# Fifth first-layer passes of two blocks as two 64-row products side by side in the array

## The reference

```python
def _L0_ffn_ref(x, Wg, bg, W1, b1, W2, b2):       # x: normalized tokens
    gate_logits = jnp.einsum('bte,en->btn', x, Wg) + bg
    top = jnp.argmax(gate_logits, axis=-1)
    h = gelu(jnp.einsum('bte,neh->nbth', x, W1) + b1)      # E=192 -> H=768
    y = jnp.einsum('nbth,nhe->nbte', h, W2) + b2           # H=768 -> E=192
    onehot = one_hot(top, N_EXP)
    return jnp.einsum('nbte,btn->bte', y, onehot)
```

## Time and profile before

| | |
|---|---|
| Median of three runs | 170.0 us |
| The profiled execution's own time | 171.58 us |
| Its span, first to last instruction | 169.8 us |
| Granted TensorE clock, mean | 0.956 of full speed |
| Busy: TensorE / VectorE / ScalarE / GpSimd | 83% / 77% / 70% / 25% |
| Costliest group on TensorE | L1414, the up passes, 360 products, 29.7 us |

### The profile page before, as it was taken

One profiled execution on the slowest core, in us unless ns is written; L12 is line 12 of the kernel. 1 busy time (PEld: TensorE's weight loads), 2 busy tenths in 40 slices (PEclk: granted clock), 3 DMA queues, 4 the chain that ended last, 5 costly groups with the idle time before them and its releaser, 6 DMA issues.

```text
span 169.8 us, 5316 instructions
## 1 busy us (share of the span) xinstructions
PE 140.6 (83%) x1893; PEld 108.5 (64%) x1893; DVE 130.3 (77%) x401; ACT 119.0 (70%) x232; POOL 42.6 (25%) x104
## 2 busy tenths in 40 slices
PE   0499588997988969988999999714899999999960
PEld 0499577974555536555657557501389999999950
DVE  2727565999999997899999896879977676767660
ACT  8934447759799985999996775560277787778610
POOL 7212522351000030101011057274001222422242
PEclk9999999999999987999999999955799999999998
DMA  3799999999999999700000012133693100101010
GB/s 83 286 297 251 257 402 256 236 226 291 367 369 368 366 367 380 314 11 0 0 4 4 4 58 109 58 130 143 187 352 122 35 30 25 29 21 37 8 46 1
DMA packets 12921, 27.72 MB, mean 163 GB/s; under 512 B 1744, under 2 KB 8666, under 8 KB 12896
## 3 DMA queue, kind: packets, MB, share of 16 engines
q1 hardware_dynamic: 11744, 24.41, 46.0%
q0 software_dynamic: 1152, 2.97, 4.8%
HBM read 15.39 MB, written 12.29 MB: 163 GB/s over the span
## 4 chain that ended last, share of the span: by engine, by line
PE 50%; DVE 15%; ACT 13%; DMA 9%; issue 8%; SPq 4%; POOL 1%; DVEq 0%; ACTq 0%; POOLq 0%
PE lin_bank L1414 12%; DMA patches<-in_patches 9%; PE head_bank L1121 4%; PE head_bank L1435 3%; PE head_bank L1427 3%; PE head_bank L1428 3%; PE lin_bank L1448 3%; PE lin_bank L1281 3%; PE lin_bank L1258 2%; ACT vint L501 2%; ACT w L519 2%; PE lin_bank L1150 2%; PE score_bank L1175 2%; PE score_bank L1281 2%; ACT aT L547 2%
## 5 line engine op out<-in xcount | busy, mean ns | idle before, releaser
L638 ACT ACTIVATE q<-lin_bank,b 128x128 f32<-128x128 f32 x72 | 25.0, 368 | 7.2 <-PE lin_bank L1414 6.5
L1414 PE MATMUL lin_bank<-q,w 128*128 128x128 f16 x360 | 29.7, 219 | 0.3 <-ACT q L628 0.3
L1121 PE MATMUL head_bank<-proj_w,patches 128*128 128x192 f32 x84 | 17.5, 368 | 8.5 <-DMA patches<-in_patches 8.4
L1414 PEld LDWEIGHTS lin_bank<-q,w 128*128 x360 | 23.7, 98 | 0.8 <-issue 0.6
L1121 PEld LDWEIGHTS head_bank<-proj_w,patches 128*128 128x128 f32 x84 | 15.9, 217 | 9.1 <-issue 6.6
L1427 PE MATMUL head_bank<-early,q 128*128 x72 | 17.7, 246 | 0.1
L1435 PE MATMUL head_bank<-early,q 128*128 x72 | 17.7, 246 | 0.0
L1428 PE MATMUL head_bank<-early,q 128*128 x72 | 17.7, 246 | 0.0
L1083 DVE CAST q<-q 128x384 f16<-128x384 f32 (+2 forms) x25 | 8.8, 352 | 11.3 <-ACT q L638 11.2
L1154 PE MATMUL lin_bank<-xqT,ww1q 96*128 96x288 bf16 x96 | 15.4, 286 | 1.6 <-ACT vint L501 0.9
L501 ACT ACTIVATE vint<-lin_bank,fac 128x768 int16<-128x768 f32 x16 | 14.3, 903 | 3.1 <-PE lin_bank L1150 2.9
(11 more groups left out here) (172 smaller groups left out, 355.2 us busy)
## 6 DMA issues: line engine op xcount, KB each, us to landing
slots<-blank SPq DMA_DIRECT2D x3, 2938.0 KB, 22.6
patches<-in_patches SPq DMA_DIRECT2D x9, 384.0 KB, 13.1
early<-in_ww SPq DMA_DIRECT2D x3, 576.0 KB, 12.0
patches<-in_w SPq DMA_DIRECT2D x4, 384.0 KB, 12.2
patches<-in_w SPq DMA_DIRECT2D x8, 192.0 KB, 13.7
patches<-in_w SPq DMA_DIRECT2D x2, 576.0 KB, 13.0
v<-slots SPq DMA_DIRECT2D x5, 226.0 KB, 3.9
patches<-slots SPq DMA_DIRECT2D x4, 226.0 KB, 4.9
```

The lines of the kernel that those rows point to most:

```text
L638: a.activation(g[:, j % 2, m], up_bank[n % 4][:, 0:P], ACT.Gelu, scale=1.0 / WSCALE, bias=b1[:, bass.ds(e, 1), m]).then_inc(g_ok, 1)
L1121: last = mm(emb_bank[t][:, 0:E], patches[:, t, kc], proj_w[:, kc], start=kc == 0, stop=kc == KE - 1)
L1414: last = mm(up_bank[n % 4][:, 0:P], up_weights(j, part, m), xT[:, j % 3, piece], start=x == 0, stop=x == len(PASSES) - 1)
```

## The change

The fifth pass's zeros go. In the rows the doubled high tail and the zeros behind the low tail are dropped (388 words instead of 452), and with them ScalarE's second copy (L541) and GpSimd's memset (L402). `slots_T` now transposes the two heads as before, and each tail twice, as 128 x 64 pieces, to PSUM partitions 0 to 63 and 64 to 127: six transposes for four. So `xT` piece 2 is as before, and piece 3 holds the low tail in both halves. For tiles 0 and 1 the fifth pass stays a full product (which now also adds low by low). For tiles 2 to 11 the high tail weights of two blocks are laid on rows 0 to 63 and on rows 64 to 127 of a new tile `tails`; the fifth passes of blocks m-1 and m are issued together after the four full passes of block m (m = 1, 3, 5), as two products of 64 rows and 128 columns into two PSUM banks. The `up` of an even block therefore ends one block later. SyncE reads the expert numbers too, behind the load of tile 2, and copies the tail weights by two DMAs for each tile, between the loads of the slot tiles. Ten slot tiles instead of eight fit into the dead buffers.

```diff
--- before
+++ after
@@ -59,10 +59,11 @@
     CENTRE_AT, GATES_AT = 5, 12
     KEEP_FROM, KEEP_TO = 2, 12
     WAVES = [(0, 4), (4, 7), (7, TT)]
-    IDX = 2 * E + TAIL
+    IDX = 2 * E
     ROW = IDX + 4
-    HI, LO = 2 * E, 2 * E + 2 * P
+    HI, LO = 2 * E, 3 * E
     QG, VG = HB // 2, PPC
+    PAIRED = 2
 
     with ExitStack() as ctx:
         def sb(name, shape, dt=F32):
@@ -195,9 +196,13 @@
 
         values = v[:].rearrange("p b n -> p (b n)").bitcast(F32)
         keys = k[:].rearrange("p b m n -> p (b m n)").bitcast(F32)
-        homes = [values[:, x * ROW:(x + 1) * ROW] for x in range(5)] + [keys[:, x * ROW:(x + 1) * ROW] for x in range(3)]
+        homes = [values[:, x * ROW:(x + 1) * ROW] for x in range(6)] + [keys[:, x * ROW:(x + 1) * ROW] for x in range(4)]
         FREE_TILES = len(homes)
         homes += [flat[:, 4 * HID + x * ROW:4 * HID + (x + 1) * ROW] for x in range(SLOT_TILES - FREE_TILES)]
+
+        t0 = 4 * HID + (SLOT_TILES - FREE_TILES) * ROW
+        tails = flat[:, t0:t0 + (SLOT_TILES - PAIRED) * HID // 4].bitcast(F16).rearrange(
+            "p (j m n) -> p j m n", j=SLOT_TILES - PAIRED, m=HM // 2)
 
         def xs(j):
             return homes[j]
@@ -229,6 +234,7 @@
         w2_in = [sem(f"w2_in{e}") for e in range(NEXP)]
         patch_in = [sem(f"patch_in{t}") for t in range(TT)]
         ww1_in = [sem(f"ww1_in{s}") for s in range(3)]
+        tail_in = [sem(f"tail_in{j}") for j in range(PAIRED, SLOT_TILES)]
         xs_in = [sem(f"xs_in{j}") for j in range(SLOT_TILES)]
         pool_step, nought_ok, ident_ok, pad_ok, qpad_ok, blank_ok, const_ok, setup, scales_ok, psum_clear = map(sem, (
             "pool_step", "nought_ok", "ident_ok", "pad_ok", "qpad_ok", "blank_ok", "const_ok", "setup", "scales_ok", "psum_clear"))
@@ -374,6 +380,14 @@
                 if j == FREE_TILES:
                     sp.wait_ge(wlo_ok, EARLY)
                 sp.dma_start(xs(j), slots_d[bass.ds(at[j], P), :]).then_inc(xs_in[j], 16)
+                if j == PAIRED:
+                    sp.wait_ge(wlo_ok, EARLY)
+                    sp.wait_ge(expert_ok, 1)
+                    experts = load_experts(mybir.EngineType.SP)
+                if j >= PAIRED:
+                    part = w1[0:TAIL, bass.ds(experts[j], 1), 2].rearrange("p e (m b n) -> p (e m) b n", b=2, n=P)
+                    for b in range(2):
+                        sp.dma_start(tails[b * TAIL:(b + 1) * TAIL, j - PAIRED], part[:, :, b]).then_inc(tail_in[j - PAIRED], 16)
 
         @block.gpsimd
         def _(pool):
@@ -399,7 +413,6 @@
             gp.iota(blank[:, IDX:ROW].bitcast(I32), pattern=[[0, 4]], base=T, channel_multiplier=1).then_inc(blank_ok, 1)
             gp.iota(row[:, :, IDX:ROW].bitcast(I32), pattern=[[P, TT], [0, 4]], base=0,
                     channel_multiplier=1).then_inc(blank_ok, 1)
-            gp.memset(row[:, :, IDX - TAIL // 2:IDX], 0.0).then_inc(const_ok, 1)
             step(gp.memset(before[:], 1.0))
 
             gp.affine_select(out=before[:], in_=before[:], compare_op=ALU.is_gt, fill=0.0, base=0,
@@ -441,7 +454,7 @@
                     pool.wait_ge(blank_out, 16 * BLANKS)
                     pool.wait_ge(const_ok, NCONST)
                 pool.wait_ge(xlo_ok, t1)
-                pool.wait_ge(xhi_ok, 2 * t1)
+                pool.wait_ge(xhi_ok, t1)
                 pool.wait_ge(slot_ok, w + 1)
                 for t in range(t0, t1):
                     gp.indirect_dma_start(out=slots_d, out_offset=bass.IndirectOffsetOnAxis(ap=slot[:, t:t + 1], axis=0),
@@ -538,7 +551,6 @@
             def norm_high(t):
                 act.wait_ge(xn_ok, t + 1)
                 a.copy(row16[:, t, HI:HI + E], xn[:, t % 2]).then_inc(xhi_ok, 1)
-                a.copy(row16[:, t, HI + E:HI + 2 * P], xn[:, t % 2, P:E]).then_inc(xhi_ok, 1)
 
             def probs_T(p):
                 act.wait_ge(aT_ps, p + 1)
@@ -909,7 +921,7 @@
                                 ALU.subtract, ALU.mult).then_inc(xn_ok, 1)
 
             def norm_low(t):
-                dve.wait_ge(xhi_ok, 2 * t + 2)
+                dve.wait_ge(xhi_ok, t + 1)
                 d.tensor_tensor(row16[:, t, LO:LO + E], xn[:, t % 2], row16[:, t, HI:HI + E],
                                 ALU.subtract).then_inc(xlo_ok, 1)
 
@@ -1378,7 +1390,9 @@
 
             def pieces(x):
 
-                return [x[:, HI:HI + P], x[:, LO:LO + P], x[:, HI + P:HI + 2 * P], x[:, LO + P:LO + 2 * P]]
+                tails = [x[:, HI + P:HI + E], x[:, LO + P:LO + E]]
+                return [(slice(0, P), 0, x[:, HI:HI + P]), (slice(0, P), 1, x[:, LO:LO + P])] + [
+                    (slice(b * TAIL, (b + 1) * TAIL), 2 + s, tails[s]) for s in range(2) for b in range(2)]
 
             def slots_T(j):
 
@@ -1386,11 +1400,15 @@
                 if j >= 2:
                     pe.wait_ge(slotT_ok, j - 1)
                 out = slotT_bank[j % 2][:, 0:2 * P].bitcast(F16).rearrange("p (s n) -> p s n", s=4)
-                for s, x in enumerate(pieces(xs(j).bitcast(F16))):
-                    last = nc.tensor.transpose(out[:, s], x, identh[:])
+                for rows, s, x in pieces(xs(j).bitcast(F16)):
+                    last = nc.tensor.transpose(out[rows, s], x, identh[:])
                 last.then_inc(slotT_ps, 1)
 
-            PASSES = [(0, 0), (0, 1), (1, 0), (2, 2), (2, 3)]
+            PASSES = [(0, 0), (0, 1), (1, 0), (2, 2)]
+
+            def tail_rows(m):
+
+                return slice(m % 2 * TAIL, m % 2 * TAIL + TAIL)
 
             def up_weights(j, part, m):
                 return w1[:, bass.ds(experts[j], 1), part, m * P:(m + 1) * P].rearrange("p e n -> p (e n)")
@@ -1405,15 +1423,30 @@
 
             def down_address(j, m):
                 nc.tensor.lower_ap(down_weights(j, m))
+
+            def up_tail(j, m):
+
+                bank = up_bank[(j * HM + m) % 4][:, 0:P]
+                if j < PAIRED:
+                    last = mm(bank, up_weights(j, 2, m), xT[:, j % 3, 3], start=False, stop=True)
+                else:
+                    last = mm(bank, tails[tail_rows(m), j - PAIRED, m // 2], xT[tail_rows(m), j % 3, 3],
+                              start=False, stop=True)
+                last.then_inc(up_ps, 1)
 
             def up(j, m):
                 n = j * HM + m
                 if n >= 4:
                     pe.wait_ge(g_ok, n - 3)
                 for x, (part, piece) in enumerate(PASSES):
-                    last = mm(up_bank[n % 4][:, 0:P], up_weights(j, part, m), xT[:, j % 3, piece],
-                              start=x == 0, stop=x == len(PASSES) - 1)
-                last.then_inc(up_ps, 1)
+                    mm(up_bank[n % 4][:, 0:P], up_weights(j, part, m), xT[:, j % 3, piece], start=x == 0, stop=False)
+                if j < PAIRED:
+                    up_tail(j, m)
+                elif m % 2:
+                    if m == 1:
+                        pe.wait_ge(tail_in[j - PAIRED], 32)
+                    up_tail(j, m - 1)
+                    up_tail(j, m)
 
             def down(j, m, following):
 
```

More of the change, by code:

```diff
@@ L24 @@
 YB = 4
-NCONST = 3 + 4 + 3 + 4 + 12 + 1 + 12 + 4 + 1
+NCONST = 3 + 4 + 3 + 4 + 12 + 1 + 12 + 4
 X1, W1Q, QQ, KQ, AQ, VQ, X2, W2Q = range(8)
```

## The result

The changed kernel takes 175.95 us, median of four runs (175.69 to 176.53), against 169.87 us (169.43 to 171.34) before it. The ratio is 1.0347 with a 95% interval of 1.0279 to 1.0416, so it is slower by 3.5%. On another chip, beside the first experiments, it was 176.81 against 170.01 us, a ratio of 1.0376 (1.0319 to 1.0433). The forecast was 176.6 us. Medians here are of all runs; a ratio is worked out over the single runs, without the few that ran slow at a lower granted clock, so it can differ from the quotient of two medians, by 0.6% at most.

A forecast was written before the change was run, and what follows sets the result against it. TensorE's gapless stream in the expert stage was taken as the bound; 4.4 + 2.1 + 0.2 + 0.2 - 0.2 - 0.1 = +6.6 us on the median of 170.0 gave 176.6 us, range 173.0 to 178.8.

The forecast's parts named there:

- What bounds the kernel: Expert stage: TensorE's stream has no gaps, 3.38 us a tile, so starts lost or gained there are in the time.
- The pairs: Tiles 2 to 11: 30 pairs of 64-row products replace full fifth passes, net +0.146 us each, +4.4 us.
- The transposes: Six for four in each `slots_T`: +0.217 us a call, 9.5 calls +2.1 us, and +0.2 for `slots_T(0)`.
- The late end: Last tile: block 4 completes later, so its GELU and the cast start later; +0.2 us, at most +0.4.
- ScalarE's copies: ScalarE's second copy, dropped nine times, mostly in slack: -0.2 us, between 0 and -1.35.
- Shorter rows: Slot tiles of 1552 instead of 1808 bytes a row: the first lands sooner, -0.1 us.
- SyncE: SyncE's queue: register read of 1.33 us and 1.5 us of issues a tile stay covered; cost 0.

The follow-up runs named there:

- each block alone: Changed kernel, but each block of tiles 2 to 11 takes its own 64-row fifth product right behind its four full passes: 183.84 us, ratio 1.0755.
- first kernel with full products alone: Against the kernel before: high and low parts laid alternately in the row, three full transposes a tile, five full passes, no tail copies: 172.62 us, ratio 1.0147.

## Why the prediction was right, by its own steps

*What bounds the kernel*, right: TensorE's stream in the expert stage, counted in starts. No other wait entered the stream.

*The pairs*, forecast +4.4 us, 4.7 by the starts: 0.010 us a pair more, since a pair's last start to the next is 0.159 where the two smaller shapes gave 0.151 for such a slot. Taking the price of shapes that are in the trace for one that isn't was the one leap, and the kernels without pairs, with one full product for a pair and with each block alone bear it out: rows alone pay as columns do. The Trainium skill (TensorEngine Tiling (Array Packing), Key Properties) says that changing the tiling mode drains TensorE. These runs agree as far as starts can tell, for 64-row tiles too: 0.21 us a round trip, whether it holds one product, two or four.

*The transposes*, forecast +2.1 and +0.2: 0.227 a call against 0.217, nine calls, +2.0. The tenth, for tile 2, is hidden whole, not half: from it to the next call is 3.87 us where it was 3.88. The stage's first pass comes 1.38 us behind its first transpose where it was 1.27, so +0.1.

*The late end*, forecast +0.2, came out at +0.1. TensorE waits before block 3 of the last tile for 0.3 us, as it did before:

```profile
165.73 0.39 PE L1442 MATMUL lin_bank<-q,w 128*128 128x128 f16 x4
166.88 0.29 DVE L1095 CAST q<-q 128x256 f16<-128x256 f32 x1
...
167.45 0.25 PE L1468 MATMUL head_bank<-early,q 128*128 x1
167.82 0.26 PE L1460 MATMUL head_bank<-early,q 128*128 x1
```

The cast starts 1.15 us behind the last block's first pass (was 0.68), but TensorE itself is 0.3 later with what it does before its wait (1.72 us behind that pass, was 1.43), and from the cast to block 3's product it took 0.94 us, was 1.10.

*ScalarE's copies*, forecast -0.2: the steps that follow the two copies on ScalarE's path come earlier by 0.14 and 0.15 us, so -0.3 by the trace.

*Shorter rows*, forecast -0.1, not seen: the first slot tile was issued at 116.17 and its transposes started at 119.20, 3.0 us later, where the kernel before has 2.65. Over all profiles the distance from VectorE's fifth low split to those transposes runs from 6.05 to 6.69 us, so no more can be said than that no gain shows.

*SyncE*, forecast 0: right in effect, wrong in size. The register read took 0.77 us, not 1.33, and each copy more than I gave it. The kernel with the copies alone shows no cost.

Sum by the starts: 4.7 + 2.0 + 0.1 + 0.1 - 0.3 = 6.6 us. From the stage's first pass on it is 4.7 + 2.0 + 0.1 = 6.8, and the two traces differ by 6.8 there. That this is the forecast's +6.6 to the tenth is partly luck: the pairs came out 0.3 above their term, and the transposes, their first call, the late end and the copies together 0.4 below theirs, with 0.1 back from the shorter rows. The medians say 6.1 us on one chip and 6.8 on the other. What the 0.7 us between them is made of stays open; executions of one kernel differ by more than that, as the clock dip shows.

## What to carry to other kernels

Count starts, not busy time, and look in your own trace for what a change of the array's shape costs: 0.21 us a round trip here, for rows as for columns, as much as four slots of 128 columns. By that price half-array products pay only if a visit saves more than that, which no kernel here reached; first ask whether both halves can be filled by laying out the operands, since a full product with two useful halves cost nothing extra here. And where addresses are computed at run time, count the queue's register operations for each block before adding an operand.

## What the runs showed of the hardware that I had not expected

TensorE's own queue can be the bound while its products look nearly full (in the first kernel with full products alone busy for 24.59 of 25 us from 125 us on, its weight loads for 20.67): four fused register operations for a block of 0.53 us cost 0.4 us a tile (3.76 us on average), and packing six addresses in three operations brought all of it back (3.33 us a tile).

At a change of the array's shape the weight load doesn't run ahead of its product: it starts some 0.004 us before it, where in the stream it starts some 0.05 to 0.08 before. The gap of 0.15 us stands in front of the load as well.

The same 1.47 us wait of TensorE is followed by a granted clock of 0.64 over 4.7 us in one execution and of 1.00 in another. The two kernels do the same TensorE work up to there, and the changed kernel alone shows both (1.00 in one profile, 0.89 over 60 to 75 us in the other); the time between is about 1.5 us. Kernels with such a wait should be compared by stages or over many runs.
